# Third layer's loop: mask product reads exponentials from PSUM in quarters, step size in the exponent, decays over the sum by broadcast DMA

## What is computed

```python
dt = softplus(dt + dt_bias)                       # per token and head
h  = h * dt[..., None]
A_cum = cumsum(A * dt)                            # within a chunk
Lmat = exp(segsum(A * dt))                        # decay from token s to token l, 0 above the diagonal
M = Gm * Lmat                                     # Gm = C_l . B_s
Y_diag = einsum('bclsh,bcshp->bclhp', M, h_c)
states = einsum('bclhn,bclhp->bchpn', B_decay, h_c)      # then a recurrence over the chunks
sdo = exp(A_cum)
Y_off = einsum('bclhn,bchpn->bclhp', C_c, states) * sdo[..., None]
y = Y_diag + Y_off + D * h_before_dt
g = y * silu(gate);  out = rmsnorm(g) * norm_w @ W_out.T
```

## Time and profile before

| | before |
|---|---|
| median of 3 runs | 1292.9 us (1292.6 to 1293.01) |
| the profiled execution's own time | 1296.16 us |
| its span, first to last instruction | 1294.4 us |
| busy: PE, DVE, ACT, POOL | 89%, 73%, 61%, 44% of the span |
| mean granted TensorE clock | 0.961 of full speed |
| the loop of the third layer | about 655 to 1105 us |

### The profile page before, as it was taken

The page is one execution under the profiler, slowest core; times in us unless marked ns, Lnnn a source line. Parts: engine busy times, 40 slices in busy tenths (PEclk is TensorE's granted clock), DMA queues, the critical chain, the costliest instruction groups (busy, mean ns, idle before and its releaser), DMA issues.

```text
span 1294.4 us, 14453 instructions
## 1 busy us (share of the span) xinstructions
PE 1150.9 (89%) x4948; PEld 615.3 (48%) x4948; DVE 939.9 (73%) x1361; ACT 795.5 (61%) x1089; POOL 573.9 (44%) x310
## 2 busy tenths in 40 slices
PE   5777999999989999998489999999999999797887
PEld 1332344444344444444266666666666666322554
DVE  4667999999955545345689999998999999323354
ACT  4567666767543334226668888888888888335542
POOL 9002899898816756230014544554454455300000
PEclk8889999999989999898699999999999999798999
DMA  3001555555422111100000000000000000000000
GB/s 121 1 1 58 192 197 178 191 180 180 174 105 82 50 41 41 41 21 0 2 15 15 15 21 15 15 22 15 15 14 22 16 15 8 1 0 1 1 1 33
DMA packets 31111, 68.48 MB, mean 53 GB/s; under 512 B 6101, under 2 KB 12022, under 8 KB 30774
## 3 DMA queue, kind: packets, MB, share of 16 engines
q1 hardware_dynamic: 31038, 67.56, 16.1%
HBM read 65.25 MB, written 1.51 MB: 52 GB/s over the span
## 4 chain that ended last, share of the span: by engine, by line
PE 41%; DVE 30%; ACT 15%; issue 7%; POOL 6%; DMA 1%; DVEq 0%; SPq 0%; POOLq 0%; ACTq 0%
DVE work L1542 7%; DVE work L1561 6%; DVE work L656 4%; PE ps L1006 4%; PE ps L1196 4%; PE ps L1022 3%; PE ps L1014 3%; POOL work L717 3%; ACT work L1403 3%; DVE yd L1606 3%; ACT work L1398 3%; PE ps L1237 2%; DVE work L1609 2%; PE ps L437 2%; ACT ps L553 2%
## 5 line engine op out<-in xcount | busy, mean ns | idle before, releaser
L1670 POOL TENSOR_TENSOR ssum<-ssum,rs 128x1024 f32<-128x1024 f32 x32 | 77.1, 2410 | 221.3 <-DVE work L1542 219.0
L656 DVE TENSOR_TENSOR_SCAN work<-ps,work 128x1024 f32<-128x1024 f32 x64 | 146.6, 2291 | 8.3
L1542 DVE SCALAR_TENSOR_TENSOR work<-work,w_t 128x1024 f32<-128x1024 f32 x96 | 123.3, 1285 | 24.0 <-ACT work L1403 21.7
L437 PE MATMUL ps<-work,ident 128*128 128x512 f32 x256 | 121.7, 598 | 5.6 <-POOL work L717 5.4
L996 POOL TENSOR_TENSOR work<-work,ssum 128x1024 f32<-128x1024 f32 x32 | 76.2, 2388 | 110.1 <-DVE work L1085 57.7
L1085 DVE TENSOR_TENSOR work<-work,ps 128x512 f32<-128x512 f32 x64 | 43.8, 687 | 99.8 <-PE ps L1014 99.8
L553 ACT ACTIVATE ps<-work,A 128x1024 f32<-128x1024 f32 x64 | 71.6, 1118 | 72.4 <-DVE work L656 72.3
L1064 ACT ACTIVATE work<-ps 128x512 f32<-128x512 f32 x64 | 38.1, 597 | 115.4 <-PE ps L1006 115.4
L717 POOL TENSOR_TENSOR work<-work 128x1024 f32<-128x1024 f32 x42 | 99.1, 2362 | 13.6 <-DVE work L656 12.3
L1678 POOL TENSOR_TENSOR yd<-yd,work 128x896 f32<-128x896 f32 x32 | 67.1, 2097 | 70.7 <-DVE work L1609 70.7
L1585 DVE SCALAR_TENSOR_TENSOR work<-work,ps 128x64 f32<-128x64 f32 x384 | 79.4, 275 | 6.3
(11 more groups left out here) (347 smaller groups left out, 2587.5 us busy)
## 6 DMA issues: line engine op xcount, KB each, us to landing
work<-bc_rows SPq DMA_DIRECT2D x42, 512.0 KB, 3.5
yd<-bc_rows SPq DMA_DIRECT2D x22, 512.0 KB, 3.6
rs<-w_rows SPq DMA_DIRECT2D x32, 256.0 KB, 4.2
ssum<-share_rows SPq DMA_DIRECT2D x32, 256.0 KB, 3.2
w_t<-in_tile_w SPq DMA_DIRECT2D x32, 195.5 KB, 2.4
work<-in_w SPq DMA_DIRECT2D x1, 2048.0 KB, 7.9
shared<-in_f SPq DMA_DIRECT2D x3, 512.0 KB, 6.1
work<-in_x SPq DMA_DIRECT2D x4, 256.0 KB, 3.7
```

Of the source, the lines that this page charges most:

```text
L437: mm = pe.matmul(ps[:, YACC + h, :], ident[:, :], HS[u % 4][:, h * BL:(h + 1) * BL], start=(n == 0), stop=(n == DS - 1))
L656: dve.tensor_tensor_scan(h, flat_pair(DABANK), h, 0.0, ALU.mult, ALU.add).then_inc(m0["scan"], 1)
L1542: c = dve.scalar_tensor_tensor(HC[u], HP[:, tap:tap + SEQ], par(u, "taps", tap), HC[u], ALU.mult, ALU.add)
L1670: pool.tensor_tensor(ssum[:, b, :], ssum[:, b, :], rs[:, :, :].rearrange("p k t -> p (k t)"), ALU.add).then_inc(m2["ss"], 1)
```

## The change

- **Exponentials stay in PSUM.** `exponentials` writes each quarter back to the BACK bank it came from. `mask_and_weigh` works in quarters of 512 elements, reads the bank, takes min(., BIG) times GT and writes LM. The banks are then laid out by head, and LM too.
- **Step size in the exponent.** ln(dt) is added to the exponent's argument of the source token (new: `LNDT`, `tiny`, `fall`; two more matmuls a chunk in the transposed sums). HDT is then h alone, copied by ACT (`turned_out`) instead of weighted by DVE.
- **Decays by DMA.** `spread_sums`, `decays_out` and `sel2` go. The decays' exponentials are made once (`decay_rows`), stored in DRAM (`sdo_rows`), and SP loads them with two broadcast DMAs of 64 x 896 a tile into Y (`load_decays`).
- The rows of the arguments also go through DRAM (`arg_rows`): three DMAs a tile instead of four. Negated copies (`nparts`, L1465) go; the split has no trip to ACT inside.

```diff
-        nparts = slot(7)[0:96, 0:T // 2].bitcast(BF16)
+        split = [parts[0:2 * H2, :], slot(7)[0:2 * H2, 0:T // 2].bitcast(BF16), parts_lo[:, :]]
+        by_head = lambda q: ps[:, BACK + q % 2, :].rearrange("p (h t) -> p h t", h=2)
@@ l2_sync @@
+            def load_decays(n):
+                b, t = divmod(n, CT)
+                if n >= 2:
+                    sp.wait_ge(m2["outp"], n - 1)
+                    sp.wait_ge(m2["sqr"], n - 1)
+                for h in range(2):
+                    sp.dma_start(Y[n % 2][h * P2:(h + 1) * P2, P:],
+                                 sdo_rows[2 * t + h:2 * t + h + 1, b * SEQ + P:(b + 1) * SEQ].to_broadcast([P2, SEQ - P])).then_inc(
+                                     (m2["sdo_in0"], m2["sdo_in1"])[n % 2], 16)
             load_tile(0)
             load_tile(1)
+            store_rows(0)
+            store_decays(0)
             sp.wait_ge(m2["rows_const"], 1)
-            sp.wait_ge(m2["act"], m2["neg"] + NB)
+            sp.wait_ge(m2["rows_out0"], 64)
             load_rows(0)
             load_rows(1)
+            store_rows(1)
+            store_decays(1)
+            load_decays(0)
+            load_decays(1)
+            sp.wait_ge(m2["rows_out1"], 64)
             for n in range(CT * BATCH - 2):
+                if n >= 1:
+                    load_decays(n + 1)
                 sp.wait_ge(m2["hc"], n + 1)
                 sp.wait_ge(m2["wo"], n + 1)
                 load_tile(n + 2)
@@ l2_pe @@
                     if q >= 2:
-                        pe.wait_ge(m2["L"], 4 * n + q - 1)
+                        pe.wait_ge(m2["M"], 4 * n + q - 1)
...
             def within_chunks(n):
-                pe.wait_ge(m2["sdo"], n + 1)
-                pe.wait_ge(m2["M"], n + 1)
+                pe.wait_ge(m2["hdt"], 2 * n + 2)
+                pe.wait_ge(m2["M"], 4 * n + 4)
...
                     turn_h(m, u1, 1)
-                    arguments(m, u1, (2,))
                     pe.wait_ge(m2["ystar"], n + 1)
                     shares(m, b1, 0)
-                    arguments(m, u1, (3,))
                     shares(m, b1, 1)
-                    spread_sums(m, b1, t1)
+                    arguments(m, u1, (2, 3))
...
             for i in range(NT):
-                mm = pe.matmul(ps[0:H2, 4 + i // 4, (i % 4) * P:(i % 4 + 1) * P], ADT[:, i, :], upper[:, :], start=True, stop=True)
+                here = slice((i % 4) * P, (i % 4 + 1) * P)
+                pe.matmul(ps[0:H2, 4 + i // 4, here], ADT[:, i, :], upper[:, :], start=True, stop=True)
+                pe.matmul(ps[H2:2 * H2, 4 + i // 4, here], LNDT[:, i, :], ident[:, :], start=True, stop=False)
+                mm = pe.matmul(ps[H2:2 * H2, 4 + i // 4, here], ADT[:, i, :], fall[:, :], start=False, stop=True)
@@ l2_act @@
+            def turned_out(n, k):
+                act.wait_ge(m2["hdd"], 2 * n + k + 1)
+                if k == 0 and n >= 1:
+                    act.wait_ge(m2["ydiag"], n)
+                act.activation(HDT[:, k * BL:(k + 1) * BL], ps[:, FRONT + k, :], ACT.Copy).then_inc(m2["hdt"], 1)
             def exponentials(n):
                 for q in range(4):
-                    if q == 3:
+                    if q == 2:
+                        turned_out(n, 0)
                         act.wait_ge(m2["st"], 2 * n + 1)
                         if n >= 1:
                             act.wait_ge(m2["yoff"], 2 * n)
                         act.activation(ST[:, 0, :], four(MID)[:, 0, :], ACT.Copy).then_inc(m2["first_state"], 1)
+                        turned_out(n, 1)
                     act.wait_ge(m2["arg"], 4 * n + q + 1)
-                    act.activation(LM[:, q * BL:(q + 1) * BL], ps[:, BACK + q % 2, :], ACT.Exp).then_inc(m2["L"], 1)
+                    act.activation(ps[:, BACK + q % 2, :], ps[:, BACK + q % 2, :], ACT.Exp).then_inc(m2["L"], 1)
@@ l2_dve @@
-            def mask_and_weigh(n, b):
-                dve.wait_ge(m2["L"], 4 * n + 4)
-                for h in range(2):
-                    part = dve.scalar_tensor_tensor(lm[:, :, h, :], lm[:, :, h, :], 1.0, GT[:, b * TB:(b + 1) * TB, :], ALU.min, ALU.mult)
-                part.then_inc(m2["M"], 1)
+            def mask_and_weigh(n, b, quarters):
+                for q in quarters:
+                    dve.wait_ge(m2["L"], 4 * n + q + 1)
+                    g = GT[:, b * TB + 2 * q:b * TB + 2 * q + 2, :].rearrange("p c l -> p (c l)").unsqueeze(1).to_broadcast([P, 2, 2 * P])
+                    dve.scalar_tensor_tensor(lm[:, :, 2 * q:2 * q + 2, :].rearrange("p h c l -> p h (c l)"), by_head(q), BIG, g,
+                                             ALU.min, ALU.mult).then_inc(m2["M"], 1)
@@ GpSimd, start of the kernel @@
-            for t in (ident_b, mask_q, zero, sel, sel2):
+            for t in (ident_b, mask_q, zero, sel):
```

More of the change, by code:

```diff
@@ L224, in build @@
         share_rows = nc.dram_tensor("share_rows", [E, T], F32, kind="Internal").ap()
+        arg_rows = nc.dram_tensor("arg_rows", [2 * H2, 3, T], BF16, kind="Internal").ap()
+        sdo_rows = nc.dram_tensor("sdo_rows", [H2, T], F32, kind="Internal").ap()
         bc_rows = nc.dram_tensor("bc_rows", [2 * DS, T], F32, kind="Internal").ap()
@@ L1176, in load_rows, with store_rows @@
-                    sp.dma_start(arg_w[r:r + 3, n % 2, :, :], nparts[of_head, here].rearrange("k (c l) -> k c l", l=P)).then_inc(rows, 16)
-                    sp.dma_start(arg_m[r + 6:r + 9, n % 2, :, h, :], parts[of_head, here].rearrange("k (c l) -> k c l", l=P)).then_inc(rows, 16)
+                    r = ROW0 + 6 + 3 * h
+                    sp.dma_start(arg_m[r:r + 3, n % 2, :, h, :], arg_rows[2 * t + h, :, here].rearrange("k (c l) -> k c l", l=P)).then_inc(rows, 16)
+            def store_rows(b):
+                sp.wait_ge(m2["dve"], m2["parts"] + (b + 1) * NB // BATCH)
+                here = slice(b * SEQ, (b + 1) * SEQ)
+                for k in range(3):
+                    sp.dma_start(arg_rows[:, k, here], split[k][:, here]).then_inc((m2["rows_out0"], m2["rows_out1"])[b], 16)
@@ L1190, in l2_sync @@
                 load_rows(n + 2)
+            load_decays(CT * BATCH - 1)
         def l2_pe(pe):
@@ L1567, in weigh @@
                 product(HDD, DEC, 0, m2["hdd"])
-                product(HDT, DT, 0, m2["hdt"])
                 dve.wait_ge(m2["tr"], 2 * n + 2)
-                product(HDT, DT, 1, m2["hdt"])
                 product(HDD, DEC, 1, m2["hdd"])
@@ L1955, in _ @@
             pool.memset(eps_t[:, :], EPS)
+            pool.memset(tiny[:, :], 1.0 / BIG)
             own(pool.memset(ident[:, :], 0.0))
@@ L1979, in _ @@
             pool.affine_select(mask_q[:, :], mask_q[:, :], [[-1, P]], ALU.is_ge, -BIG, base=0, channel_multiplier=1)
-            for t, w in ((sel2, P2), (sel, P)):
-                for k in range(3):
-                    ins = pool.affine_select(t[:, :, :], t[:, :, :], [[-1, H2], [0, w]], ALU.not_equal, 1.0,
-                                             base=-H2 * k, channel_multiplier=1)
-                    if k == 2 and w == P:
-                        ins.then_inc(const["ready"], 1)
-                    else:
-                        own(ins)
+            for k in range(3):
+                ins = pool.affine_select(sel[:, :, :], sel[:, :, :], [[-1, H2], [0, P]], ALU.not_equal, 1.0,
+                                         base=-H2 * k, channel_multiplier=1)
+                if k == 2:
+                    ins.then_inc(const["ready"], 1)
+                else:
+                    own(ins)
             l0_pool(pool, own)
```

89 lines of the change are left out of this document (47 added, 42 removed).

## The result

The changed kernel takes **1302.03 us** (median of 20 runs, 1293.77 to 1306.33), the kernel before, on the same chip, 1294.01 (20 runs, 1288.72 to 1297.63): ratio 1.0054, 95% interval 1.0041 to 1.0068. It is slower by 0.5%; 1270 was forecast, and the range of 1264 to 1284 does not hold it. One single execution, of the kernel with half of the decays, took 2314 us for a reason that nothing here shows, and is left out.

The account below looks back on a forecast made before the run. A ring through DVE, PE and ACT bounds the 14.02 us step; the change makes it 13.3, set by the second ring. Loop -22.3, ahead +0.9, start -1.6: -23.0 off the median 1292.9, 1270 us, range 1264 to 1284.

Parts of the forecast that it names:

- d: Time on SP's queue from the first decay issue to the landing of the tile's weights, taken as 4.2 us.
- the second ring: Third layer's loop: output matmuls' end, decays and weights on SP's queue, projection, filters; 4.72 + d + 0.1 + 4.25 = 13.27 us.
- Rival 2: SP's queue takes over the step from d = 5.15; at d = 5.4, 14.45 a step, 1302 us; chance 0.06.
- The nearest pair: Earlier trace's broadcasts of 512 KB, landing in 3.5, and 256 KB behind, in 4.2 + 0.37; basis for d.
- First ring: Third layer's loop, compute path from filters to projection (8.85) and back to filters (4.25): 13.1 us a step.
- the two branches said to meet: Before the projection, DVE's masks with the argument matmuls and ACT's exponentials with copies both end at 8.85 after the filters' start.
- Mask quarters: DVE's mask product in the loop as four of 512 out of PSUM, 0.62 to 0.69 each, 2.5 to 2.75 us.
- First, switch and last period: Loop's edge periods: first 0.9 shorter, batch-half change 0.85 longer, last filters to last yd 1.1 shorter.
- Ahead of the loop: Before the third layer's loop: cumulative sums +3.7, split -2.8, together +0.9 us, up to +4.6.
- rival 3: Ahead of the loop, the cumulative sums don't overlap: +3.7 us, 1274; chance 0.10.
- The start, -1.6: Kernel's start: without sel2's selects on POOL, DVE's last L260 takes 0.69; saves 1.6 us (0 to 3.3).
- rival 4: In the loop, DMA is not late at all (d under 4.0): 13.1 a step, 1264 us; chance 0.61 together with the forecast.

## Why the prediction was wrong

**The step that failed** is the size of d in the second ring: "I take d = 4.2". It was 4.83 at best in an ordinary step and 5.17 in the mean. The mechanism and its place (SP's queue) were in the prediction, and its remainder nearly so: 9.22 instead of 9.07. With 0.05 for the one step at a lower clock, 5.17 + 9.22 + 0.05 gives the 14.44. Rival 2 priced the slowest case, d = 5.4, as 14.45 a step and 1302 us, and 14.44 and 1302.03 came. That the two meet so closely is partly luck: d was 0.23 shorter than its 5.4, and the remainder 0.2 longer. The rival was given 0.06, with the words that it "needs the slowest landing every time". It did not: 1.19 of issues and an ordinary landing of 3.98 were enough.

Where the 0.97 between 4.2 and 5.17 come from:
- *The issues.* Two of 0.37 were counted. They take 1.19 up to the weights' own issue (961.51 to 962.70): +0.45. The price came from issues of other shapes: in the trace of the kernel before, a broadcast over 128 rows took 0.32 to 0.43, but the rows of the arguments (L1176, L1177) 0.67 to 0.80. An issue of a 64-row broadcast is 0.45 to 0.60, and the weights' own rises from 0.36 to 0.54 when it stands behind them.
- *The landing.* The 4.2 leaves 3.46 for the weights from their issue to their landing; it measured 3.9 in the median, 3.98 in the mean of the ordinary steps and up to 5.2: +0.52. The nearest pair, 512 and 256 KB, was read as an upper case because of its bytes. Half the bytes gave 3.2, none ahead 2.6: the row of a lone transfer (2.4) plus a share for what is ahead.
- *No slack.* The two rings cross at d = 3.98. The forecast of 4.2 lay close above that edge, where an error upwards counts in full and one downwards hardly at all: every 0.1 more is 28 x 0.1 = 2.8 us. The range stopped at d = 4.7, while the trace's own pair (4.2 + 0.37) and its slowest (5.4) bracketed 5.17.

The rule of the Trainium skill that was weighed, "DMA: Bandwidth & Descriptors", on HWDGE ordering (a semaphore increment lands only after every earlier write of its DMA engine), agrees with the runs: the weights are reported 2.6 after issue with nothing just ahead, 3.2 behind half of the decays, 3.9 behind all. A mere sharing of the DMA engines would give such landings too; no run tells the two apart. The prediction's estimate from the Trainium skill's fixed 2.0 us and HBM limit, 3.8 for both loads together, does not agree: 4.83 and more were measured. The Trainium skill gives the 2.0 us in its section "Anatomy of one DMA" for the GpSimd path, and these loads are SP's. The estimate also counts nothing for the issues, of which 1.19 stand ahead of the weights' own.

**Point by point, what held:**
- *First ring, 13.1*: 13.20 with the weights first, at 8.94 + 4.26 where 8.85 + 4.25 was worked out. Of the two branches said to meet, the chain of waits names the argument matmuls; ACT's second copy ends 0.15 before the projection, at 962.70. DVE's idle before the filters there is 1.00, not 0.7.
- *Mask quarters 0.62 to 0.69, exponentials into PSUM as before*: starts 0.60 apart (two in 1.28), mean 681 ns; exponentials 580 ns against 596 ns into SBUF. The errata rule of the Trainium skill's "VectorE: DVE Perf Modes", 62 cycles more for a PSUM source, gave 2.6 for the four quarters (an estimate); from start to start they take 4 x 0.60 = 2.4. No run reads the same quarters out of SBUF, so the 62 cycles themselves are not measured.
- *First, switch and last period*: 0.83 shorter (predicted 0.9), 0.88 longer (0.85), 1.25 shorter (1.1). From the first weighted product to the first filters 7.18 against 7.98, 0.80 shorter (0.9).
- *Ahead of the loop*: the cumulative sums overlap and the projection behind them starts at 630.49 (predicted: sums end near 630.4), so rival 3 is out. The split takes (638.32 - 631.22)/4 = 1.78 a block (1.9). From the first scan to the loop's first weighted product it is 0.2 longer (0.9 forecast). In the timelines of PE and DVE:

```profile
630.18 0.38 PE L1362 MATMUL ps<-fall,work 128*32 128x128 f32 x2
630.49 1.98 PE L1235 MATMUL ps<-work,w_t 128*128 128x512 f32 x4
```

```profile
631.22 0.68 DVE L1570 TENSOR_TENSOR rs<-ps,parts 64x512 f32<-64x512 f32 x1 [6.32 <-ACT parts L1501]
...
638.32 7.75 DVE L1409 SCALAR_TENSOR_TENSOR work<-work,vec 128x1024 f32<-128x1024 f32 x6
```

- *The start, -1.6*: L265 takes 0.69, and the input's last maximum starts 1.54 earlier (28.49 against 30.03). Right as a term, and too large in the sum: about 0.6 of it is left at the first scan, since TensorE mostly ran the next large group at a lower granted clock.
- The forecast without the second ring (rival 4, 1264) plus 28 x 0.1 is 1267: what the kernel with the weights first gives.

The traces also explain two oddities. Single steps that take much longer (16.76 once; 17.34, 17.57 and 16.00 with four DMAs) are those in which a late landing is followed by a lower granted clock. The first period of the loop is 14.90 in some traces and 16.07 in others, of the same program too (14.90 and 16.07 with the weights first): PE idles 2.26 there for ACT in all of them. The turning matmuls behind that wait take 273 ns where the period is 14.90, and 417 to 421 where it is 16.06 or 16.07, at a granted clock of 0.71 over 665 to 670 with the weights first, second time.

**Open.** Why a single landing takes 5.2. Whether the decays in another queue, but issued at the same moment as the weights, would hold them back: the run meant for it did not place them there. It was not tried whether the kernel before with the decays ahead of its weights is slower as well.

## What to carry to other kernels

When a change puts transfers ahead of another on a queue that is refilled from inside the loop, close that ring first: the event that releases the queue, every issue at its own shape's price, the landing behind those writes, and the compute back to the event. If it lands within a tenth or two of the compute ring, forecast from the upper bound, since errors count on one side only. And try the free remedy: the load that is wanted first is issued first, and the one with a whole step of slack goes behind it; here that order was worth 35 us, from 1302 to 1267.

## What the runs showed of the hardware that was not expected

- SP takes 0.45 to 0.60 us to issue one broadcast DMA of 64 rows, and 0.54 instead of 0.36 for the same 128-row load directly behind two of them. The time of the broadcasts did not depend on the bytes: 1.09 for two of 224 KB and for two of 112 KB.
- A load's landing grows with what was issued just ahead on its queue: 2.6 with nothing, 3.2 behind 224 KB, 3.9 behind 448 KB (medians). It also depends on how long ago that was issued: 3.1 behind the same 448 KB in four DMAs, whose issues take 2.46.
- DVE's product of two SBUF tiles (L260) takes 3.66 instead of 0.69 us while POOL runs a select, and ends 0.5 behind it (28.20, the select 27.66). Without the select there it takes 0.69. This holds in every trace of each kind. The earlier start that this gave PE was partly lost again to a lower granted clock (8.1 to 8.7 us for the matmuls that take 7.03).
- The same wait of TensorE does not always have the same effect on its clock: behind 2.26 us of idle time at the loop's start the matmuls took 273 ns in seven traces (the kernel before among them) and 417 to 421 ns in four.
